# Scores of two cross-attentions as one pass of 96 contraction rows, with stacked operands built by on-chip transfers

## The reference

```python
q = split_heads(query @ Wq + bq); k = split_heads(bank @ Wk + bk); v = split_heads(bank @ Wv + bv)
scores = einsum('bhqd,bhkd->bhqk', q, k) / sqrt(32)
out = einsum('bhqk,bhkd->bhqd', softmax(scores), v)      # then out @ Wo + bo
```

## Time and profile before

| what | value |
|---|---|
| device time, median of 3 runs | 2616.84 us (2612.31 to 2621.23) |
| profiled execution, first to last instruction (span) | 2613.8 us |
| PE busy | 2432.4 us, 93% |
| DVE, ACT, POOL busy | 1110.8 (42%), 947.7 (36%), 585.1 us (22%) |
| TensorE granted clock, mean | 0.934 |
| all DMA queues | 93.6 MB |

### The profile page before, as it was taken

One profiled execution on the slowest core, in us unless ns is written; L12 is line 12 of the kernel. 1 busy time (PEld: TensorE's weight loads), 2 busy tenths in 40 slices (PEclk: granted clock), 3 DMA queues, 4 the chain that ended last, 5 costly groups with the idle time before them and its releaser, 6 DMA issues.

```text
span 2613.8 us, 38193 instructions
## 1 busy us (share of the span) xinstructions
PE 2432.4 (93%) x14208; PEld 2160.2 (83%) x14208; DVE 1110.8 (42%) x2206; ACT 947.7 (36%) x1892; POOL 585.1 (22%) x397
## 2 busy tenths in 40 slices
PE   4899999999977789699999999998999999999997
PEld 3788888888866667588888888887999999999997
DVE  7455545555457368444556455654640000200022
ACT  2444434454443144343454344533222222311130
POOL 4111101110132634311111011101222222222222
PEclk9899999999978878789999999998999999999998
DMA  3000000000021010100100000000111111111111
GB/s 136 1 24 24 15 8 23 23 23 6 22 81 29 1 44 0 60 1 28 28 27 21 6 27 27 32 1 33 64 48 65 56 64 56 56 56 64 56 57 41
DMA packets 29513, 93.60 MB, mean 36 GB/s; under 512 B 3752, under 2 KB 4008, under 8 KB 29320
## 3 DMA queue, kind: packets, MB, share of 16 engines
q1 hardware_dynamic: 29448, 92.72, 11.0%
HBM read 91.07 MB, written 1.64 MB: 35 GB/s over the span
## 4 chain that ended last, share of the span: by engine, by line
PE 86%; DVE 6%; ACT 3%; POOL 3%; issue 2%; DMA 0%; DVEq 0%; SPq 0%; POOLq 0%; ACTq 0%
PE psS L272 18%; PE psS L274 16%; PE psS L273 16%; PE psT L1337 7%; PE psJ L272 4%; PE psJ L273 4%; PE psJ L274 4%; PE psO L272 4%; PE psO L274 3%; PE psO L273 3%; PE psT L272 2%; PE psT L274 2%; PE psT L273 2%; DVE x_res L884 1%; DVE stats L877 1%
## 5 line engine op out<-in xcount | busy, mean ns | idle before, releaser
L272 PE MATMUL psS<-hid_hi,fw_hi 128*128 128x400 f32 x1152 | 398.1, 346 | 15.4 <-DVE hid_lo L1258 10.6
L274 PE MATMUL psS<-hid_hi,fw_lo 128*128 128x400 f32 x1152 | 400.2, 347 | 0.0
L273 PE MATMUL psS<-hid_lo,fw_hi 128*128 128x400 f32 x1152 | 399.6, 347 | 0.0
L529 POOL TENSOR_TENSOR fw_lo<-raw,fw_hi 128x1024 fp32r<-128x1024 f32 x88 | 216.7, 2464 | 572.1 <-ACT fw_hi L751 572.1
L615 ACT ACTIVATE pT_hi<-psT 128x300 fp32r<-128x300 f32 x512 | 187.4, 418 | 263.0 <-PE psT L1337 262.5
L1258 DVE TENSOR_TENSOR hid_lo<-h_act,hid_hi 128x800 fp32r<-128x800 f32 x32 | 32.3, 1083 | 555.6 <-ACT hid_hi L840 555.6
L606 ACT ACTIVATE p<-psS,nmax 100x722 f32<-100x722 f32 x256 | 221.9, 867 | 68.9 <-DVE nmax L928 36.4
L936 DVE TENSOR_TENSOR pT_lo<-psT,pT_hi 128x300 fp32r<-128x300 f32 x512 | 216.4, 464 | 38.1 <-ACT pT_hi L615 32.8
L370 POOL TENSOR_TENSOR cT_lo<-ctx_raw,cT_hi 128x722 fp32r<-128x722 f32 x58 | 102.1, 1761 | 580.0 <-ACT cT_hi L565 580.0
L272 PEld LDWEIGHTS psS<-hid_hi,fw_hi 128*128 128x128 f32 x1152 | 218.0, 189 | 16.4 <-issue 11.2
L272 PE MATMUL psO<-pT_hi,vv_hi 128*64 128x200 f32 (+1 forms) x768 | 219.2, 285 | 2.4 <-DVE oraw L947 2.4
(11 more groups left out here) (306 smaller groups left out, 4909.4 us busy)
## 6 DMA issues: line engine op xcount, KB each, us to landing
raw<-ffn_dram SPq DMA_DIRECT2D x88, 512.0 KB, 3.2
ctx_raw<-ctxT_dram SPq DMA_DIRECT2D x60, 361.0 KB, 3.1
mask_raw<-mask_dram SPq DMA_DIRECT2D x8, 282.0 KB
raw<-wk_dram SPq DMA_DIRECT2D x4, 512.0 KB, 3.5
raw<-wv_dram SPq DMA_DIRECT2D x4, 512.0 KB, 6.6
raw<-wq_dram SPq DMA_DIRECT2D x4, 512.0 KB, 3.3
raw<-wo_dram SPq DMA_DIRECT2D x4, 512.0 KB, 3.2
cin<-xT_dram SPq DMA_DIRECT2D x1, 1600.0 KB, 8.3
```

The lines of the kernel that those rows point to most:

```text
L272: nc.tensor.matmul(out, st[0], mv_[0], start=first, stop=False)
L273: nc.tensor.matmul(out, st[0], mv_[1], start=False, stop=False)
L274: return nc.tensor.matmul(out, st[1], mv_[0], start=False, stop=last)
L529: nc.gpsimd.tensor_tensor(fw.lo[:, e, :], raw[:, e, :], fw.hi[:, e, :], ALU.subtract)\
```

## The change

Let q = qh + ql and k = kh + kl. Where there were three passes of 32 contraction rows, there is one of 96: the stationary operand is qh, qh, ql stacked over partitions 0 to 95 and the moving one kh, kl, kh. Rows can't be moved between partitions by PE-side indexing, so the stacks are built by DMA:

- Keys: `kT` keeps one group instead of two. `key_stack` issues for each group 3 x 4 DMAs, each of 32 partitions x 722 floats (92 KB), SBUF to SBUF, into `kS` (two groups deep).
- Queries: each projected unit (128 x 400) is split by DVE into two small buffers, and `queries_out` issues three DMAs per unit that store the parts in a DRAM tensor, in rows of 100 floats; 24 DMAs for an attention. `query_stack` loads one group of one batch back with 3 DMAs, in rows of 100 floats, into `qS` (two groups deep). `queries_hi` and `queries_lo` go.
- Keys are projected at other steps: group 2 in steps 1 and 2, group 3 in 7 and 8, the next batch's group 0 in 14 and 15, its group 1 between the last value projections. The context's high parts are at t = 10, 11, 12, 13.
- SP's stream has per batch 4 x 15 stack DMAs between the context loads. `rows` keeps one bias row and is loaded three times.

```diff
-CONTEXT_AT = {10: 0, 11: 1, 13: 2, 14: 3}
+CONTEXT_AT = {10: 0, 11: 1, 12: 2, 13: 3}
+KEYS_AT = {1: (0, 2, 0), 2: (0, 2, 1), 7: (0, 3, 0), 8: (0, 3, 1), 14: (1, 0, 0), 15: (1, 0, 1)}
+STACK = 3
+GROUP_IN = 16 * STACK * (G + 1)
...
+        kS = at("kS", [STACK * HD, 2, G, KEYS], f32r)
...
+        qS = at("qS", [STACK * HD, 2, G, T], f32r)
...
+        q_dram = [nc.dram_tensor(f"q_dram{L}", (NB, C, STACK, G, HD, T), fp32, kind="Internal").ap() for L in range(2)]
...
+            def queries_out(L):
...
+                for i in range(2 * C):
+                    m, h = i // 2, i % 2
+                    sp.wait_ge(a.q_lo, i + 1)
+                    for part, t in enumerate((q_parts.hi, q_parts.hi, q_parts.lo)):
+                        sp.dma_start(q_dram[L][h * NB // 2:(h + 1) * NB // 2, m, part].rearrange("b j r t -> (j r) b t"),
+                                     t[:, i % 2, :].bitcast(fp32).rearrange("p (b t) -> p b t", t=T))\
+                          .then_inc((a.q_out0, a.q_out1)[i % 2], 16)
+
+            def query_stack(L, b, g):
...
+                wait(sp, a.s_mm, H * b + G * (g - 1))
+                for part in range(STACK):
+                    sp.dma_start(qS[HD * part:HD * (part + 1), g % 2, :, :].bitcast(fp32),
+                                 src[:, g, part].rearrange("a j r t -> r (a j) t"))\
+                      .then_inc((a.stack0, a.stack1)[g % 2], 16)
+
+            def key_stack(L, b, g):
...
+                sp.wait_ge(a.k_lo, 8 * b + (2 * g + 2))
+                for part, t in enumerate((kT.hi, kT.lo, kT.hi)):
+                    for j in range(G):
+                        sp.dma_start(kS[HD * part:HD * (part + 1), g % 2, j, :].bitcast(fp32),
+                                     t[HD * j:HD * (j + 1), :].bitcast(fp32))\
+                          .then_inc((a.stack0, a.stack1)[g % 2], 16)
+
+            def first_stacks(L):
+                a = A[L]
+                sp.wait_ge(a.q_out0, 48 * C)
+                sp.wait_ge(a.q_out1, 48 * C)
+                query_stack(L, 0, 0)
+                query_stack(L, 0, 1)
+                key_stack(L, 0, 1)
...
+                def batch(b, last):
+                    if not last:
+                        context(a, b + 1, range(2))
+                    for g in range(2, C):
+                        query_stack(L, b, g)
+                        key_stack(L, b, g)
+                    if not last:
+                        context(a, b + 1, range(2, C))
...
+                        for g in range(2):
+                            query_stack(L, b + 1, g)
+                            key_stack(L, b + 1, g)
...
-                dst = kT.hi[:, g % 2, k0:k0 + kn]
+                if i == 0:
+                    wait(act, (a.stack0, a.stack1)[(g + 1) % 2], GROUP_IN * (2 * b + (g + 1) // 2))
+                dst = kT.hi[:, k0:k0 + kn]
...
+            def queries_split(L):
+
+                a = A[L]
+                for i in range(2 * C):
+                    dve.wait_ge(a.q_done, i + 1)
+                    wait(dve, (a.q_out0, a.q_out1)[i % 2], 48 * (i // 2))
+                    nc.vector.tensor_copy(q_parts.hi[:, i % 2, :], qf[:, i % 2, :]).then_inc(q_hi, 1)
+                    dve.wait_ge(q_hi, 2 * C * L + i + 1)
+                    nc.vector.tensor_tensor(q_parts.lo[:, i % 2, :], qf[:, i % 2, :], q_parts.hi[:, i % 2, :],
+                                            ALU.subtract).then_inc(a.q_lo, 1)
...
                 def scores(b, h):
                     g, j = divmod(h, G)
-                    if h == 0:
-                        pe.wait_ge(a.qs_done, b + 1)
                     if j == 0:
-                        pe.wait_ge(a.k_lo, 8 * b + 2 * g + 2)
+                        pe.wait_ge((a.stack0, a.stack1)[g % 2], GROUP_IN * (2 * b + g // 2 + 1))
...
-                        mm = three(psS[h % 2][0:T, k0:k0 + kn], (qs.hi[rows_, g, :], qs.lo[rows_, g, :]),
-                                   (kT.hi[rows_, g % 2, k0:k0 + kn], kT.lo[rows_, g % 2, k0:k0 + kn]), True, True)
+                        mm = nc.tensor.matmul(psS[h % 2][0:T, k0:k0 + kn], qS[:, g % 2, j, :],
+                                              kS[:, g % 2, j, k0:k0 + kn], start=True, stop=True)
```

More of the change, by code:

```diff
@@ L106, in decoder_kernel @@
         resid = at("resid", [T, 2, D], fp32)
-        rows = at("rows", [T, 3, D], fp32)
+        rows = at("rows", [T, D], fp32)
         sel = at("sel", [H, C, P], fp32)
@@ L316, in _ @@
+                with nc.sync.Fori(0, NB - 1) as b:
+                    batch(b, False)
+                batch(NB - 1, True)
             sp.dma_start(cols[:, :], d["cols"]).then_inc(conv_in, 16)
@@ L413, in batch @@
                             split_lo(n, i, FFN0_W[n])
[L414 removed]
+                    add_bias(b, None, base + b, a.resid_done)
                 batch(0, False, first=True)
@@ L625, in batch @@
                             exps(b, t)
-                        g, i = t // 4 + 1, t % 4
-                        if i < 2 and g < C and t < 12:
+                        ahead, g, i = KEYS_AT.get(t, (2, 0, 0))
+                        if ahead == 0:
                             keys_hi(L, b, g, i)
-                        if t >= H - 1 and not last:
-                            keys_hi(L, b + 1, 0, t - H + 1)
+                        if ahead == 1 and not last:
+                            keys_hi(L, b + 1, g, i)
                         if t in CONTEXT_AT and not last:
@@ L690, in _ @@
             queries(A[0], True)
-            act.wait_ge(A[0].q_done, 2 * C)
-            queries_hi(A[0], 0)
+            for i in range(2):
+                keys_hi(0, 0, 1, i)
             for i in range(2):
@@ L809, in _ @@
             queries(A[1], False)
-            act.wait_ge(A[1].q_done, 2 * C)
-            queries_hi(A[1], 0)
+            for i in range(2):
+                keys_hi(1, 0, 1, i)
             for i in range(2):
@@ L1067, in _ @@
                 transposed_lo(LN_CONV + b, b)
+            queries_split(0)
+            for i in range(2):
+                keys_lo(0, 0, 1, i)
             attention(0, LN_ATT0)
@@ L1225, in _ @@
                 values_lo(A[1], 0, j)
+            queries_split(1)
+            for i in range(2):
+                keys_lo(1, 0, 1, i)
             attention(1, LN_ATT1)
@@ L1360, in batch @@
                             weighted(b, (t - 3) // 2, (t - 3) % 2)
-                        g, i = t // 4 + 1, t % 4
-                        if i < 2 and g < C and t < 12:
+                        ahead, g, i = KEYS_AT.get(t, (2, 0, 0))
+                        if ahead == 0:
                             keys(a, b, g, i)
-                        if t >= H - 1 and not last:
-                            keys(a, b + 1, 0, t - H + 1, fresh=t == H - 1)
+                        if ahead == 1 and not last:
+                            keys(a, b + 1, g, i, fresh=i == 0)
                     if not last:
@@ L1381, in batch @@
                     if not last:
-                        for j in range(3, NKC):
-                            values(a, b + 1, j)
+                        values(a, b + 1, 3)
+                        values(a, b + 1, 4)
+                        keys(a, b + 1, 1, 0)
+                        values(a, b + 1, 5)
+                        keys(a, b + 1, 1, 1)
                     if isinstance(b, int) and b == 0:
@@ L1421, in _ @@
             queries(A[0], wqo)
+            for i in range(2):
+                keys(A[0], 0, 1, i)
             attention(0, LN_ATT0)
@@ L1558, in _ @@
             queries(A[1], wqo)
+            for i in range(2):
+                keys(A[1], 0, 1, i)
             attention(1, LN_ATT1)
```

107 lines of the change are left out of this document (58 added, 49 removed).

## The result

The changed kernel takes 2644.1 us (median of 4 runs, 2642.4 to 2646.5) against 2618.2 us for the kernel before, run beside it: ratio 1.0097, 95% interval 1.0082 to 1.0113. I had forecast 2590, that is 1% faster. The time lies outside the forecast's own range (2560 to 2615) and inside the one with the rivals (2515 to 2665); the sign is wrong. The profiled execution has a span of 2644.6 us, 30.8 more than before.

The account below looks back on a forecast made before the run. PE's work, 93% busy, was taken as the bound. Span 2613.8 - 20 (batches) - 35 (clock) + 27 (queries) = 2586; median 3.0 over span: 2589, said as 2590 us; own range 2560 to 2615, with rivals 2515 to 2665.

Parts of the forecast that it names:

- Step 1: Score passes removed: a new head takes 0.49 us and saves 0.67, 10.7 us a batch over 16 heads.
- Step 2: Steps without keys: the loop over ACT's exponential limits them to 2.40 us instead of 2.65; PE idles 3.8 us a batch.
- Step 3: Head 0 of each batch: about 2.85 us from first scores to transposes, 1.95 us of it idle.
- Step 5: Key stacks: twelve copies issued at 0.445 us, late 0.3 at head 12 and 1.3 at group 2; 1.6 us a batch.
- Rival B: Key stacks late in every batch, issues at 0.6 us, 60 us lost: 2650 us; chance 0.17.
- Step 8: PE's clock: falls in 5 of 16 batches instead of some 13, 35 us gained; bounds 56 gained or 60 lost.
- Rival D: Clock falls as often as before, because of head 0's idle stretch, 35 us less gained: 2625 us; chance 0.13.
- Step 9: Queries through DRAM at each attention's start: 40 ns a row, 3.8 us a unit, 13.6 us later, twice 27 us.
- Rival C: Query stores of 400 B are dear, 64 ns a row, 6.1 us a unit: 2627 us; chance 0.12.
- step 6: Third context load: 1.0 us late a batch, so PE waits; lower bound 0 if head 12's wait covers it.
- step 7: Second attention: longer maximum makes DVE need 2.4 to 2.45 us a head; 0.8 us a batch there, 0.4 on average.
- Step 4: DVE behind keys: the maximum starts late after steps 2 and 8, delaying the next transposes; 1.3 us a batch.

Follow-up runs that it names:

- e9: Kernel before with one score pass of 96 rows read in place instead of three of 32, no transfers, scores wrong: 2525.0 us, ratio 0.9651.
- e2: Changed kernel with 3 of 12 key copies per group, all four heads reading the first head's stack: 2600.4 us, ratio 0.9936.
- e5: Changed kernel with the queries' DRAM tensor reordered so that a stored row has 1600 B instead of 400: 2625.7 us, ratio 1.0024.
- e10: Changed kernel with e5's rows and query loads counted on semaphores of their own: 2608.7 us, ratio 0.9963.
- e14: Changed kernel with e2, e10 and 16 unread passes ahead of head 0's transposes together: 2546.2 us, ratio 0.9733.
- e4: Changed kernel with 16 passes that nobody reads ahead of head 0's transposes: 2640.1 us, ratio 1.0082.
- e13: e12 without the 16 unread passes ahead of head 0's transposes: 2586.6 us, ratio 0.9891.
- e1: Kernel before with one score pass of 32 rows instead of three, two products left out: 2605.1 us, ratio 0.9936.
- e3: Changed kernel with key copies of 512 columns instead of 722: 2634.9 us, ratio 1.0054.
- e12: Changed kernel with e10, e4's passes, GpSimd issuing low-part copies behind the bias, earlier group 1 keys, SyncE awaiting high parts only: 2565.2 us, ratio 0.9804.
- e6: Changed kernel with the four low-part key copies of each group issued by GpSimd instead of SyncE: 2665.8 us, ratio 1.0184.

## Why the prediction was wrong

**Where the time went.** Without transfers the pass of 96 rows gives 94 us (e9). Late stacks take 44 of them back (e2), stores of 400 B 18 (e5), the shared semaphore 17 (e10). The change as it is lies 119 above e9. These three are 79 of it, the 21 between e14 and e9 another part; the 19 left are what appears only when the parts are mended together, e14's 16 passes among it. The edits overlap in what they free, so this is an account by differences and not a split into causes.

**Step 1, right in kind.** Transposes follow the scores by 0.34 us where nothing waits (325.68 to 326.02 after), not 0.49; so a step with keys saves 0.15 more than forecast.

**Step 2, right.** 329.56 to 332.03 is 2.47 us, forecast 2.40, and transposes wait for ACT's exponential in each such step. But the clock did fall inside these steps, at head 4 in two batches and at head 10 in four, which the prediction had named as a sign of being wrong.

**Step 3, short.** First scores to first transposes 3.69 us, forecast 2.85, because the maximum starts 1.57 behind the scores, after the last batch's residual add. 0.8 us a batch, some 13 us over 16 of them. The idle stretch is 2.87 us in most batches of the first attention and 3.1 to 3.6 in most of the second, forecast 1.95.

**Step 5 failed, the first of two.** "SP issues two DMAs in 0.89 us, 0.445 each" is right for loads and was taken for copies inside SBUF, which take 0.62. From the last key pass to the scores that need it: forecast 8.5 us, measured 10.5 (325.68 to 336.18). At head 12 the forecast of 0.3 us late, 5 in 16 batches, became 38.8. At group 2's second half 1.3 became 1.69 in the batch shown, but 0.5 or none in most; there the clock had fallen at head 0 before, and PE's longer passes took the time (e4 has 1.7 to 3.2 in each batch of the first attention). That term was also summed wrongly: its parts as written give 8.5 + 0.6 + 0.6 = 9.7 us against 2.8 + 2.85 + 0.5 + 2.0 + 1.0 = 9.15, 0.5 late and not 1.3. Rival B had the cause, issues at 0.6, and got 0.17. That its 2650 lies near 2644 is in part luck: it charged 3.8 us a batch for two places, and one of the two is late in every batch; the rest of the miss came from the clock and the starts.

**Step 8 failed, the second.** "5 of 16 still falling, 35 us gained": all 16 fell, most of them twice, at head 0 and at head 12. Rival D (2625, chance 0.13) had the first place right; no rival had the second, which follows from step 5. e4 shows that filling head 0 alone gives little as long as the stacks are late, e13 that it gives 21 us when they are not. Set against one pass of 32 rows, the gain from 96 rows was real and larger than my bound of 56 (e1 against e9: 80), and was lost again to waits.

**Step 9, one term failed.** The first scores come 21.6 us later than before behind the first query pass (43.8 against 22.2), not 13.6. The stores run nearly as forecast, 3.5 us a unit (88.38 to 112.88 for seven) against 3.8, though not for the reason given: a row takes 31 ns of an engine and not 40, and DVE waits for the two small buffers, 31.2 us in 12 waits. (The lower bound of 32 ns comes to 15 us by the step's own numbers, not 17.) "Less 4.0 for group 1's keys, which PE does meanwhile" is wrong: ACT, which must empty those keys, waits for the query loads on the shared semaphore. e10 takes that away. Rival C, dear stores, is in the landing (3.9 to 4.6 instead of 1.5), and e5 shows it.

**Steps 4, 6, 7.** The context's late load (step 6) is not seen in the change, as its lower bound had it: head 12's wait covers it. With that wait gone it appears: ACT waits for context loads 28 times in e2, 20.1 us in all, and 30 times in e14, 20.9 us, near the 1.0 us a batch of step 6. The second attention's batches are not longer than the first's (82.5 against 83.1), but their granted clock is higher (0.95 against 0.93) and PE is idle 12.3 us in each against 11.8. In e9, where both have 0.98 but for one batch, the second's have 0.4 us more idle time. So about half of step 7's 0.8 was there. Step 4 was not tested alone.

**Left open.** Why e3 gains 9 us, and where e10 gains the 6 us behind the second start. Why some batches of e12 keep the clock and others with nearly the same waits lose it at head 4 or 10. Whether the numbers multiplied, and not the rows alone, count in e1 against e9.

## What to carry to other kernels

Before counting on a transfer's cover, find a row for the issue of that very kind of transfer and multiply it by their number; twelve copies at 0.62 us are 7.5 us of issuing. Where PE is the bound, price each new wait twice, as idle time and as the clock behind it, and expect little of the clock back while another such wait is left (4 us beside late stacks, 21 without them). Count transfers for different readers on different semaphores, or the earliest reader waits for the latest transfer.

## What the chip showed that I had not expected

- The same passes with 32 and with 96 contraction rows: clock 0.908 against 0.947 over the span, batches of 80 to 90 against 77 to 80 us (e1, e9). The passes themselves are not dearer: at a clock of 1.00 the next pass starts 0.23 us behind one of 512 columns and 96 rows, and 0.31 behind a head's first one of 32 rows (e9 and e1; in the earlier trace rows the second of 32 rows has 0.23 too).
- SP takes 0.62 us to issue a copy of 32 partitions inside SBUF, whatever its columns (512 or 722); 0.445 for a load from DRAM. GpSimd takes 0.5 us (four in 1.97). With both engines issuing, copies land 2.8 to 3.3 us after their issue instead of 2.1 (e6, e12). The Trainium skill (DMA: Bandwidth & Descriptors, "Rules for kernel authors") says that spreading DMAs over engines gives no bandwidth and saves issue time only; e6 and e12 agree: the landings did not get shorter, and head 12 came 2 us a batch sooner, since issue time was what was short.
- Stores with rows of 1600 B land in 2.1 us, with rows of 400 B in 3.9, for the same 200 KB (e5).
